# Second attention started while the experts run: tiles by rank of rows, results stored in place

## The chip, the cores and the metric

One core of a Trainium2 chip runs one program: TensorE (PE), VectorE (DVE), ScalarE (ACT), GpSimd (POOL) and the DMA queue engine SP. The metric is device time in microseconds; the kernel before took 1532.71 us (median of 3 runs, 1528.11 to 1534.6).

## The reference, cut to what matters

The input is 16 batches of 256 tokens of 128 numbers, all float32. Four blocks, each followed by a residual sum and a layer norm:

```
x = LN(x + attention0(x))    # MLP, 16 heads of 64, softmax over keys j < i + 64, output projection
x = LN(x + experts(x))       # 16 experts of 128 -> 512 -> 128 with exact gelu, top 4 of 16 per token
x = LN(x + attention1(x))    # 16 heads of 8, LoRA-corrected q, k, v, o; keys of the own batch
x = LN(x + gated(x))         # per batch t: f, i = sigmoid, g = tanh of x_t and state c;
                             # c = f*c + i*g over t = 0..15; h = tanh(x_t wo + c_final uo + bo)
```

The router's logits are minus the squared distance to 16 keys plus a linear term; the weights of the four best are a softmax over them. The state c (256 x 128) is carried over all 16 batches, and the last block's output needs the final c for every batch.

## The kernel before, in words

All of it is one program with an instruction stream for each engine, written out by hand; semaphores (`need`, `need_alone`, `wait_ge`) set the order. It has four stages.

**First attention** (loops over 16 batches x 8 pairs of heads, `body(b)` of each engine). When a batch is normed, DVE routes it: `pos` is the row of `xs` (in HBM; a region of CAP = 4224 rows for each expert) of each of the token's four copies, and POOL scatters the 256 x 4 rows there with eight indirect DMAs (L515). SP fills `xs` with zeros beforehand.

**Experts.** Once all rows are scattered, DVE makes a plan (L1284 to L1315): 144 tiles of 128 rows, all tiles of expert 0 first, then those of expert 1, and so on. For tile n, SP loads the rows (L408), PE transposes them (L850), DVE copies that expert's weights out of `wall` (L1348, L1351) and the transposed rows out of PSUM (L1355), PE does the first layer (L864), ACT the gelu (L1076), PE two tiles later the second layer (L873), DVE adds the bias (L1376), SP stores pairs of tiles to `ys` (L414). The loop has a body of 24 tiles (TURN), five of them straight code and three passes of a loop in the middle. POOL meanwhile shifts all positions from regions to plan order (L552 to L566), clears the stacks and builds constants, each piece released by a tile (`next_tile`).

**Second attention** (`attention_loop`: bodies b = -3 to 17, the middle ones in a loop of three). Body b works on several batches at once: POOL gathers batch b+5 (eight indirect DMAs, L614), ACT weighs batch b+4 (L1136), POOL sums it (L640 to L644), DVE norms batch b+3 (`norms_start`, `norms_end`), PE projects batch b+2 to q and k (L925, L926), which are split in three bf16 parts (`parts`) and sent by SP through HBM (`qkd`, L439) into stacks `qst`, `kst` (L447 to L451), PE computes scores of batch b+1 (L967) for their row maxima (L1389), and of batch b transposed, with the maxima as further rows of the stack (L892), of which ACT takes the exponential (L1086) and PE the product with v (L904). The maxima travel as `mrow` (ACT L1141), then by a DMA of SP into 24 rows of the stack (L459), once for each half of the heads: half 1 is needed at the body's pair p = 4, half 0, sent at p = 5 of the body before, at its first pair. Batch b-1 gets its output projection and norm, batch b-2 its gates (L983 to L987), and POOL updates the state (L650 to L656).

**Tail.** PE multiplies the last state (L994), DVE adds it and POOL a quarter (L1477, L677), ACT takes tanh in four groups of four batches (L1151), DVE and POOL add the residual (L1484, L681), DVE and POOL compute the last norm's moments, ACT scales (L1156) and SP writes out.

## Time and profile before

| | |
|---|---|
| median of 3 runs | 1532.71 us |
| profiled execution | 1530.1 us, span 1528.3 us |
| busy share PE, DVE, ACT, POOL | 83%, 66%, 61%, 52% |
| mean granted TensorE clock | 0.93 |
| mean DMA | 76 GB/s, 115.51 MB |

The profile's times count from the start of the span. An engine's idle time is put down to what released it; "issue" is time in which it waited for nothing that the profile shows. A line such as L864 is a line of the kernel. `wall` as a target in the second attention is the third stack and the exponentials: they lie in the place of the experts' weights.

### The profile page before, as it was taken

The page shows a single profiled execution, that of the slowest core. Times are in us where ns is not written, and L with a number is a line of the kernel's source. Part 1 is how long each engine was busy: PE and PEld are TensorE (multiplying, and loading weights), DVE is VectorE, ACT ScalarE, POOL GpSimd, SP SyncE. Part 2 cuts the span into 40 slices and gives each one's busy share as a digit, 9 for nine tenths or more (in the row PEclk, how much of TensorE's full clock was granted, in tenths as well). Part 3 has the DMA queues.
Part 4 walks back from the last instruction along what each step waited for, and adds up shares of the span by engine and source line. Part 5 has one row for each costly group of instructions (what it writes and reads, how often), then busy time and mean ns, then how long its engine had stood idle before and what let it go on. Part 6 is the DMA issues. An engine that isn't in the chain of part 4 may idle for free.

```text
span 1528.3 us, 36861 instructions
## 1 busy us (share of the span) xinstructions
PE 1270.1 (83%) x9712; PEld 970.9 (64%) x9712; DVE 1011.6 (66%) x3751; ACT 939.1 (61%) x2828; POOL 796.6 (52%) x1025
## 2 busy tenths in 40 slices
PE   7999999999999999856999889803768787878870
PEld 3776767777777776646999889801445554555540
DVE  2677777777777777755776657514677776668726
ACT  5877777777777777624665456412555655656544
POOL 1557777777777777743332100175456665653133
PEclk9999999999999999978999999955899999999995
DMA  9522222222222222112222122115343435343201
GB/s 345 171 60 70 69 67 67 69 69 69 69 69 69 69 69 69 44 51 58 72 69 70 58 61 70 56 45 92 82 86 74 94 66 91 68 88 57 46 4 55
DMA packets 150448, 115.51 MB, mean 76 GB/s; under 512 B 11809, under 2 KB 139937, under 8 KB 148290
## 3 DMA queue, kind: packets, MB, share of 16 engines
q1 hardware_dynamic: 142146, 97.50, 24.9%
q0 software_dynamic: 8192, 16.79, 4.2%
q8 instruction: 39, 0.64, 0.2%
q14 instruction: 71, 0.58, 0.1%
HBM read 50.02 MB, written 61.08 MB: 73 GB/s over the span
## 4 chain that ended last, share of the span: by engine, by line
PE 29%; DMA 7%; DVE 5%; issue 4%; DVEq 3%; POOL 2%; ACT 2%; another core or an unknown queue 2%; SPq 1%; POOLq 1%; ACTq 0%
PE psum L864 8%; PE psum L873 8%; DMA qst<-mrow 3%; DMA wall<-mrow 3%; PE psum L904 2%; PE psum L892 2%; PE psum L967 2%; POOL yk L614 1%; PE psum L983 1%; PE psum L850 1%; DVE mx L1389 1%; PE psum L984 1%; ACT wall L1086 1%; DMA yk<-ys,posc 1%
## 5 line engine op out<-in xcount | busy, mean ns | idle before, releaser
L525 POOL TENSOR_SCALAR P<-P,rinv 128x192 f32<-128x192 f32 (+1 forms) x384 | 309.4, 820 | 154.1 <-DVE rinv L1216 151.7
L1051 ACT ACTIVATE P<-shifted,least 128x192 f32<-128x192 f32 (+1 forms) x512 | 240.2, 471 | 103.2 <-DVE least L1202 101.8
L1076 ACT ACTIVATE hid<-psum,wA 128x128 f32<-128x128 f32 x576 | 164.7, 369 | 118.9 <-PE psum L864 118.9
L1389 DVE TENSOR_REDUCE mx<-psum 128x2 f32<-128x512 f32 x256 | 165.0, 686 | 83.4 <-PE psum L967 56.1
L1086 ACT ACTIVATE wall<-psum 128x1024 f32<-128x1024 f32 x128 | 131.1, 1024 | 98.9 <-PE psum L892 81.7
L1202 DVE CUSTOM_DVE_ANT_0 shifted<-psum,band 128x192 f32<-128x192 f32 (+1 forms) x512 | 168.7, 384 | 26.0 <-PE psum L749 25.7
L864 PE MATMUL psum<-xgT,wA 128*128 128x128 f32 x1152 | 155.8, 279 | 8.9 <-DVE xgT L1355 8.8
L515 POOL DMA_INDIRECT xs<-x1c,pos x128 | 128.2, 1001 | 56.8 <-issue 28.3
L873 PE MATMUL psum<-wB,hid 128*128 128x128 f32 x1152 | 153.5, 277 | 0.0
L614 POOL DMA_INDIRECT yk<-ys,posc x128 | 124.2, 970 | 55.7 <-issue 29.0
L864 PEld LDWEIGHTS psum<-xgT,wA 128*128 128x128 f32 x1152 | 143.4, 196 | 9.6 <-issue 9.5
L873 PEld LDWEIGHTS psum<-wB,hid 128*128 128x128 f32 x1152 | 141.5, 194 | 0.0
L786 PEld LDWEIGHTS psum<-ident,P 128*128 128x128 f32 x1024 | 117.0, 141 | 36.3 <-issue 29.4
L786 PE MATMUL psum<-ident,P 128*128 128x128 f32 x1024 | 134.9, 274 | 3.7 <-POOL P L525 1.5
L749 PE MATMUL psum<-kT,qT 64*128 64x192 f32 (+1 forms) x1024 | 131.5, 375 | 0.6 <-DVE least L1202 0.6
L804 PE MATMUL psum<-PT,V 128*64 128x256 f32 (+1 forms) x1024 | 112.2, 362 | 0.7 <-DVE PT L1190 0.7
L749 PEld LDWEIGHTS psum<-kT,qT 64*128 64x128 f32 x1024 | 80.2, 186 | 38.6 <-issue 36.9
L1348 DVE COPY wA<-wall 128x516 f32 x144 | 61.9, 430 | 64.4 <-ACT hid L1076 41.5
L1051 ACT ACTIVATION_READ_ACCUMULATOR P<-shifted,least 128x1 f32 x512 | 95.9, 187 | 0.0
L1190 DVE COPY PT<-psum 128x448 f32<-128x448 f32 x128 | 79.0, 618 | 17.1 <-PE psum L804 7.8
L697 PE MATMUL psum<-hT,wg 128*128 (+1 forms) x256 | 88.9, 429 | 1.7 <-ACT kT L1008 0.9
L804 PEld LDWEIGHTS psum<-PT,V 128*64 128x64 f32 x1024 | 68.5, 138 | 30.9 <-issue 9.0
(243 smaller groups left out, 2550.7 us busy)
## 6 DMA issues: line engine op xcount, KB each, us to landing
xs<-zrow SPq DMA_DIRECT2D x33, 1024.0 KB
xg<-xs SPq DMA_DIRECT2D x144, 64.0 KB, 1.8
ys<-yrow SPq DMA_DIRECT2D x72, 128.0 KB, 1.9
wall<-in_wall SPq DMA_DIRECT2D x1, 8232.0 KB, 36.5
qkd<-parts SPq DMA_DIRECT2D x32, 192.0 KB
qst<-qkd SPq DMA_DIRECT2D x66, 64.0 KB
wall<-qkd SPq DMA_DIRECT2D x35, 64.0 KB
kst<-qkd SPq DMA_DIRECT2D x11, 192.0 KB
```

The costliest lines, as they stand in the source:

```text
L525: g.tensor_scalar(x, x, rinv[:, par, n:n + 1], None, ALU.mult).then_inc(s["pn_ready"], 1)
L614: g.indirect_dma_start(out=yk[:, slot, count * half + n, :], out_offset=None, in_=ys, in_offset=bass.IndirectOffsetOnAxis(posc[:, half, n: ...
L749: last = mm(bk[:, c0:c0 + w], qT[64 * h:64 * h + 64, p, it * 128:(it + 1) * 128], kT[64 * h:64 * h + 64, p, 0:w], start=True, stop=True)
L786: last = nc.tensor.transpose(bk[:, c0:c0 + 128], P[:, par1, it, h, jt * 128:(jt + 1) * 128], ident[:, :])
L804: last = mm(OTB[64 * h:64 * h + 64, k * N + c0:k * N + N], V[:, jt, r * 128 + 64 * h:r * 128 + 64 * h + 64], PT[:, k, h, keys], start=(jt ...
L864: mm(UP[two][:, at:at + GT], wA[:, p % 4, f * 128:(f + 1) * 128], xgT[:, p % 4, :], start=True, stop=True).then_inc(s["up_mm"], 1)
L873: last = mm(DN[two][:, 0:D], hid[:, m, f, :], wB[:, m, f * D:(f + 1) * D], start=(f == 0), stop=(f == FC - 1))
L1051: last = sc.activation(P[:, par, it, h, 0:w], shifted[:, par, it, h, 0:w], ACT.Exp, scale=-1.0, bias=least[:, par, n:n + 1], accum_out=row ...
L1076: sc.activation(hid[:, p % 4, f, :], UP[two][:, at:at + GT], ACT.Gelu, bias=wA[:, p % 4, F + f:F + f + 1]).then_inc(s["hid_ready"], 1)
L1086: sc.activation(pc[:, p % 4, :, :, :].rearrange("q h j n -> q (h j n)"), ST, ACT.Exp, scale=SCALE1).then_inc(s["exps1"], 1)
L1202: v.tensor_tensor_reduce(out=shifted[:, par, it, h, 0:w], in0=bk[:, c0:c0 + w], in1=band[:, it, 0:w], scale=-SCALE0, scalar=3.0e38, op0=AL ...
L1389: v.tensor_reduce(out=mx[:, :, h], in_=SB[(par + 1 + h) % 3].rearrange("q (i n) -> q i n", i=TT), axis=mybir.AxisListType.X, op=ALU.max).t ...
```

## The change

What it does, by part:

- The plan goes by rank: first the first tile of every expert, then every second tile, and so on (`upto`, `level`, `order`). Rows no longer change place: results are stored into the rows of `xs` that were read, tile by tile, and `pos` is used as it is; POOL's shift of positions is gone. Empty tiles get rows of their own behind the regions.
- The experts' loop is straight code of 144 tiles. Their hidden layer takes three PSUM banks in turn instead of four (`up`), which frees bank 7.
- During the experts POOL gathers batches 0 to 3 (once 32, 64, 96 and 128 tiles are stored), ACT weighs and POOL sums batches 0 to 2, DVE norms batches 0 and 1, PE transposes them and projects batch 0, and SP loads its stack. The second attention then begins with body -1 instead of -3.
- Before the experts: no barrier of four engines; the last batch's rows go to `h1` instead of `x1c`; its pow stands ahead of two scatters; ACT loads the table of gelu early.
- In the second attention the DMA of `mrow` is issued by ACT, in `maxima_row`; `parts` go out in four DMAs of 64 partitions instead of two of 128; the transposes of x2 and x3 stand behind the last scores of a body; POOL adds `bo2` to each batch's output rows.
- Tail: for the last two batches DVE updates the state; the last gates compute the part without c ahead; output rows are put into PSUM by an identity matmul and the state's part is added there, tanh reads PSUM; the last scaling is shared by ACT and DVE.

The diff, cut to its core:

```diff
-TURN = 24
-NT += -NT % TURN
-ROWS = DUMMY + GT
+NT += NT % 2
+FULL = TOK * TOPK // GT
+ROWS = DUMMY + (NT - FULL) * GT
+LEVELS = TOK // GT
...
+        def up(n, f):
+            return bank[(2 * n + f // 2) % 3][:, (f % 2) * GT:(f % 2 + 1) * GT]
...
+            def store_rows(n):
+                need_alone(sp, "yrow_ready", n + 1)
+                need_alone(sp, f"ys_out{n % 2}", 16 * (n // 2))
+                sp.dma_start(xs[bass.ds(row[n], GT), :], yrow[:, n % 4, :]).then_inc(s[f"ys_out{n % 2}"], 16)
...
+            sp.wait_ge(s["scat"], 16 * B * TT * TOPK)
+            for n in range(NT + 4):
+                if n + 4 < NT:
+                    load_rows(n + 4)
+                if n >= 4:
+                    store_rows(n - 4)
+                if n == 95:
+                    store_parts(-2)
...
+                if n in (98, 100, 102):
+                    load_stack(-2, 0, (n - 98) // 2)
...
-            for e in range(E):
-                for half in (slice(0, npos // 2), slice(npos // 2, npos)):
-                    next_tile()
-                    g.tensor_scalar(shift[:, half, e], posf_all[:, half], first_row[:, e:e + 1], delta[:, e:e + 1], ALU.is_ge, ALU.mult)
...
+            stored(32)
+            fetch(-5, -5 % 3, 0)
+            fetch(-5, -5 % 3, 1)
+            combine_ahead(-4, 60)
+            stored(64)
...
+            stored(128)
+            fetch(-2, -2 % 3, 0)
+            fetch(-2, -2 % 3, 1)
             pool.wait_ge(s["wB_ready"], NT)
             clear(2)
             select_copy(2)
             g.drain().then_inc(s["cleared"], 1)
-            pool.wait_ge(s["ys_out"], 8 * NT)
+            stored(NT)
...
+            for n in range(NT + 2):
+                tile(n)
+                if n == 82:
+                    attention(-3, -3 % 3, (7,))
+                if n == 86:
+                    attention(-2, -2 % 3, (1,))
+                if n == 116:
+                    attention(-2, -2 % 3, (7,))
...
                 need_full(act, b, use)
                 sc.activation(mrow[:, half, :], shared(use).bitcast(bf16)[0:NMAX, 0:N], ACT.Copy).then_inc(s[f"free{use[0]}"], 1)
...
+                act.dma_start(qst[slot][MROW:MROW + NMAX, half * hh:half * hh + hh, :],
+                              mrow[:, half, :].rearrange("q (o n) -> q o n", o=1).to_broadcast([NMAX, hh, N])).then_inc(s["mrow_in"], 16)
...
+            for n in range(NT):
+                tile(n)
+                if 50 <= n < 58:
+                    weigh_ahead(-4, n - 50)
+                if n == 83:
+                    attention(-3, -3 % 3, (7,))
+                if 85 <= n < 93 and n != 87:
+                    weigh_ahead(-3, n - 85 - (n > 87))
...
-            v.tensor_tensor_scan(ncum[:, :], past[:, :], ntile[:, :], 0.0, ALU.mult, ALU.add)
+            v.tensor_tensor(lesser[:, :, :], ntile[:, :].rearrange("q (o e) -> q o e", o=1).to_broadcast([128, LEVELS, E]),
+                            levels[:, :].rearrange("q (l o) -> q l o", o=1).to_broadcast([128, LEVELS, E]), ALU.min)
+            v.drain()
+            v.tensor_reduce(out=upto[:, :], in_=lesser[:, :, :], axis=mybir.AxisListType.X, op=ALU.add)
...
+            for n in range(NT + 2):
+                tile(n)
+                for b, first in ((-3, 70), (-2, 104)):
+                    if n == first:
+                        norms_start(b)
...
+            def state_in(c):
+
+                wo3 = gu[:, 3, :].rearrange("q (o d) -> q o d", o=1).to_broadcast([128, 2, D])
+                for half in range(2):
+                    for it in range(TT):
+                        last = mm(bank[2 * c + half].rearrange("q (k i d) -> q k i d", k=2, i=TT)[:, :, it, :], c2[:, it * 128:(it + 1) * 128], wo3, start=False, stop=(it == TT - 1))
+                last.then_inc(s["h_full"], 1)
```

The change moves instructions; three places show how. First SP in the second attention, one body that loads a stack (`qkd` is the split q and k in HBM, `mrow` the row maxima, `wall` here the third stack). Before:

```order
L439 DMA qkd<-parts 128x3x256 x2
L447 DMA kst<-qkd 24x4096
L449 DMA qst<-qkd 8x4096 x3
L447 DMA kst<-qkd 16x4096
L449 DMA qst<-qkd 8x4096 x2
L447 DMA kst<-qkd 8x4096
L449 DMA qst<-qkd 8x4096
L451 DMA qst<-zeros 24x4096
L459 DMA wall<-mrow 24x8x256 x2
```

And now:

```order
L440 DMA qkd<-parts 64x3x256 x4
L451 DMA kst<-qkd 24x2x2048
L453 DMA qst<-qkd 8x2x2048 x3
L451 DMA kst<-qkd 16x2x2048
L453 DMA qst<-qkd 8x2x2048 x2
L451 DMA kst<-qkd 8x2x2048
L453 DMA qst<-qkd 8x2x2048
L455 DMA qst<-zeros 24x2x2048
```

The two DMAs of `mrow` have left SP's queue, and the parts go out in four. Second, ACT in a body of the second attention, from the exponential of pair 4 on (`tf`, `ti` are gates, `yk` the gathered rows that it weighs). Before:

```order
L1108 ACTIVATE tf<-psum,gcol 128x256
L1109 ACTIVATE ti<-psum,gcol 128x256
L1086 ACTIVATE wall<-psum 128x1024
L1141 ACTIVATE mrow<-psum 24x256
L1086 ACTIVATE wall<-psum 128x1024
L1090 ACTIVATE oTc<-psum 128x256
L1112 ACTIVATE tg<-psum,gcol 128x256
```

And now:

```order
L1206 ACTIVATE tf<-psum,gcol 128x256
L1207 ACTIVATE ti<-psum,gcol 128x256
L1185 ACTIVATE wall<-psum 128x1024
L1237 ACTIVATE mrow<-psum 24x256
L1240 DMA qst<-mrow 24x8x256
L1185 ACTIVATE wall<-psum 128x1024
L1189 ACTIVATE oTc<-psum 128x256
L1210 ACTIVATE tg<-psum,gcol 128x256
```

The DMA of `mrow` stands on ACT behind the copy that makes it. Third, PE in the experts around tile 82 (L913 is the first layer, L924 the second, L1004 the transposes of batch 0's norm). Before, the tiles go on unbroken:

```order
L864 MATMUL psum<-xgT,wA 128x128 x4
L850 MATMUL psum<-ident,xg 128x128
L873 MATMUL psum<-wB,hid 128x128 x4
L864 MATMUL psum<-xgT,wA 128x128 x4
L850 MATMUL psum<-ident,xg 128x128
L873 MATMUL psum<-wB,hid 128x128 x4
```

And now:

```order
L913 MATMUL psum<-xgT,wA 128x128 x4
L901 MATMUL psum<-ident,xg 128x128
L924 MATMUL psum<-wB,hid 128x128 x4
L1004 MATMUL psum<-ident,x2c 128x128 x2
L913 MATMUL psum<-xgT,wA 128x128 x4
L901 MATMUL psum<-ident,xg 128x128
L924 MATMUL psum<-wB,hid 128x128 x4
L913 MATMUL psum<-xgT,wA 128x128 x4
```

The transposes, which opened the second attention before, stand between two tiles.

## Rows read from the trace of the kernel before

**Rows 1.** The page, part 2: granted TensorE clock in 40 slices.
```profile
PEclk9999999999999999978999999955899999999995
```

**Rows 2.** Busy time by stretch of the whole core (from:to, length, then as headed).
```profile
core 0: us, PE busy (x) PEld busy (x) DVE busy (x) ACT busy (x) POOL busy (x), PEclk, DMA share, GB/s
835.00:850.00 15.00, 10.34 (x74) 10.16 (x73) 6.71 (x21) 4.68 (x16) 2.91 (x6) 0.77 0.15 45
850.00:885.00 35.00, 35.00 (x316) 35.00 (x316) 23.70 (x72) 21.45 (x76) 2.37 (x5) 1.00 0.23 68
885.00:905.00 20.00, 15.90 (x128) 15.72 (x128) 10.43 (x33) 8.40 (x30) 0.00 (x0) 0.91 0.18 52
988.00:1044.00 56.00, 3.40 (x8) 1.76 (x8) 7.72 (x26) 7.49 (x24) 38.21 (x50) 0.54 0.28 60
1044.00:1068.00 24.00, 10.70 (x45) 5.05 (x46) 17.20 (x38) 6.58 (x19) 13.51 (x17) 0.64 0.45 84
1067.90:1452.80 384.90, 306.55 (x2544) 204.32 (x2544) 275.19 (x824) 224.46 (x442) 198.79 (x268) 0.92 0.39 74
```

**Rows 3.** Timeline before the first tile (start, length, engine, line, operation, idle).
```profile
672.48 0.75 POOL L506 TENSOR_TENSOR rstd<-veps,minus_half 128x2 f32<-128x2 f32 x1
...
674.41 0.60 DVE L1262 TENSOR_SCALAR x1c<-res,mv,rstd 128x128 f32<-128x128 f32 x2 [0.52 <-DMA xs<-x1c,pos]
...
692.10 0.96 POOL L515 DMA_INDIRECT xs<-x1c,pos  x1 [0.30 <-issue]
...
699.97 1.94 PE L864 MATMUL psum<-xgT,wA 128*128 128x128 f32 x8
...
701.13 1.28 ACT L1076 ACT_TABLE_LOAD   x1 [13.90 <-PE psum L864]
```

**Rows 4.** Timeline from the last tile to the first scores.
```profile
987.94 0.29 DVE L1376 TENSOR_TENSOR yrow<-psum,wB 128x128 f32<-128x128 f32 x1 [0.60 <-PE psum L873]
...
1044.01 1.04 PE L967 MATMUL psum<-kst,qst 128*128 128x256 bf16 x4 [6.40 <-DMA qst<-zeros]
```

**Rows 5.** Timeline of PE: starts of seven bodies of the second attention.
```profile
1067.94 1.04 PE L892 MATMUL psum<-qst,kst 128*128 128x256 bf16 x4 [6.90 <-DMA qst<-mrow]
...
1172.74 0.61 PE L892 MATMUL psum<-qst,kst 128*128 128x256 bf16 x4 [1.34 <-ACT wall L1086]
...
1197.24 0.61 PE L892 MATMUL psum<-wall 128*128 128x256 bf16 x4 [1.36 <-ACT wall L1086]
...
1223.10 1.03 PE L892 MATMUL psum<-qst,kst 128*128 128x256 bf16 x4 [3.65 <-DMA qst<-mrow]
...
1303.85 0.61 PE L892 MATMUL psum<-qst,kst 128*128 128x256 bf16 x4 [1.22 <-ACT wall L1086]
...
1331.08 0.61 PE L892 MATMUL psum<-qst,kst 128*128 128x256 bf16 x4 [1.22 <-ACT wall L1086]
...
1452.84 0.60 PE L892 MATMUL psum<-qst,kst 128*128 128x256 bf16 x4 [0.33 <-ACT wall L1086]
```

**Rows 6.** Timeline of SP: three issues in the second attention.
```profile
1208.88 0.33 SPq L447 DMA_DIRECT2D kst<-qkd  x1
...
1212.95 0.84 SPq L459 DMA_DIRECT2D qst<-mrow  x1
...
1447.93 9.41 SPq L459 DMA_DIRECT2D qst<-mrow  x2
```

**Rows 7.** The page, part 6: KB each, median us to landing.
```profile
xg<-xs SPq DMA_DIRECT2D x144, 64.0 KB, 1.8
ys<-yrow SPq DMA_DIRECT2D x72, 128.0 KB, 1.9
```

**Rows 8.** Timeline of the tail.
```profile
1489.42 0.41 POOL L650 TENSOR_SCALAR tf<-tf 128x256 f32<-128x256 f32 x1 [5.75 <-ACT tg L1112]
...
1493.11 1.22 PE L994 MATMUL psum<-gu,c 128*128 128x128 f32 x4 [4.40 <-POOL c L656]
...
1500.52 1.21 DVE L1484 TENSOR_TENSOR x_all<-x_all,wall 128x1024 f32<-128x1024 f32 x1
```

More of the change, by code:

```diff
@@ L69, in attention_loop @@
 def attention_loop(eng, body):
-    for b in range(-3, 3):
+    for b in range(-1, 3):
         body(b, b % 3)
@@ L416, in _ @@
[L416 to L427 removed]
+                row[n] = row_of(n)
@@ new lines, in load_stack @@
+            def load_stack(b, load, qa):
+                if qa == 0:
+                    need_alone(sp, "qkd_out", 64 * (b + 3))
+                    need_alone(sp, "st_full", 8 * b)
+                rows = [qkd[w].rearrange("e a (d h) n -> (a d) e (h n)", h=H1 // 2) for w in range(2)]
+                q, k = [x[load].rearrange("q (e h) n -> q e (h n)", e=2) for x in (qst, kst)]
+                count = NPART - qa
+                n = sum(NPART - c for c in range(qa))
+                sp.dma_start(k[DH1 * n:DH1 * (n + count), :, :], rows[1][0:DH1 * count, :, :]).then_inc(s["stk"], 16)
+                for m in range(count):
+                    sp.dma_start(q[DH1 * (n + m):DH1 * (n + m + 1), :, :], rows[0][DH1 * qa:DH1 * (qa + 1), :, :]).then_inc(s["stk"], 16)
+                if qa == NPART - 1:
+                    sp.dma_start(q[MROW:MROW + NMAX, :, :], no_maxima).then_inc(s["stk"], 16)
@@ L883, in attention @@
+            def attention(b, par, steps=range(8)):
                 nxt = (par + 1) % 3
-                for p in range(8):
+                for p in steps:
                     if has(b, 0):
@@ new lines, in outputs_in @@
+            def outputs_in(c):
+                need(pe, "xo_kept", 4 * (c + 1))
+                if c == 0:
+                    need(pe, "exps1", 8 * B)
+                if c in (1, 2):
+                    need(pe, "max_done", H1 * B)
+                if c == 2:
+                    need(pe, "o_free", 4 * B)
+                    need(pe, "to_free", 4 * B)
+                if c == 3:
+                    for k in range(2):
+                        need(pe, f"free{k}", tally[k].before(B + 2))
+                for half in range(2):
+                    mm(bank[2 * c + half][:, :], ident[:, :], xo_all[:, 8 * c + 4 * half:8 * c + 4 * half + 4, :].rearrange("q t d -> q (t d)"), start=True, stop=False)
@@ L1121, in attention @@
                         if has(b, 3):
-                            last = sc.activation(x2T[:, par, :], shared(TX)[:, 0:N], ACT.Copy)
+                            last = sc.activation(x2T[:, par, :], shared(TX, b)[:, 0:N], ACT.Copy)
                         if has(b, -1):
-                            last = sc.activation(x3T[:, :], shared(TX)[:, N:2 * N], ACT.Copy)
+                            last = sc.activation(x3T[:, :], shared(TX, b)[:, N:2 * N], ACT.Copy)
                         last.then_inc(s[f"free{TX[0]}"], 1)
-                    if p == 7 and isinstance(b, int) and b == -3:
-                        for half in range(2):
-                            weigh(b, par, half)
             def weigh(b, par, half):
@@ L1457, in attention @@
                         norms_start(b)
+                        norms_spread(b)
                     if p == 6 and (has(b, 3) or has(b, -1)):
                         norms_end(b)
+                        norms_out(b)
                     if p == 2 and has(b, 2):
-                        need(dve, "a1_ready", b + 3)
-                        v.tensor_tensor(rest[:, :], shared(QK)[:, :], parts[:, 0, :], ALU.subtract).then_inc(s[f"free{QK[0]}"], 1)
+                        for k in range(3):
+                            parts_of(b, k)
```

659 lines of the change are left out of this document (359 added, 300 removed).

## Prediction

> **What bounds the kernel now.** I read the busy slices and the clock row first, then busy time by stretch, then timelines of the stretches in which TensorE idles, and last the issue table. The clock row shows two dips, at slices 18 (the hand-over to the experts) and 27 to 29 (from the experts to the second attention) [rows 1]. TensorE does the experts at full rate: 316 instructions in 35.00 us is 9.03 per us; a tile is 17 instructions (two times 4 matmuls of two passes, one transpose), so 1.88 us, and 144 tiles are 271 us [rows 2]. Two stretches fall short: 74 instructions in 15 us and 128 in 20 us [rows 2]. From 988 to 1044 us TensorE runs 8 instructions, POOL is busy 38.21 us [rows 2]: the gathers. So the kernel is four stages in series, each with another limit: the first attention (not changed), the experts (TensorE), the second attention (no engine over 306.55 of 384.90 us [rows 2], a ring of waits), and a tail on DVE and ACT. The change works on the seams and on the ring of waits.
>
> The sum is made against the profiled execution, 1530.1 us with a span of 1528.3. The median shown is 1532.71, within 0.2% of it, so I give the sum as the forecast.
>
> **Before the first tile.** The last batch's pow stood on POOL behind two scatters of batch 14 that now follow it. One scatter is 0.96 us and a gap of 0.30 [rows 3], so 2.5 us sooner; the pow ended at 673.2 and DVE wrote x1c at 674.41 with 0.52 us idle for scatters that still read x1c [rows 3], which goes too, since these rows now go into h1. Positions are released before gates are written, about 0.5 more. From the end of the last scatter, 693.06, to the first tile's matmul at 699.97 are 6.9 us [rows 3]. They held the landing, a four-engine barrier, DVE's small set-up, weight copies and a load of rows (1.8 us [rows 7]). The barrier, set-up and weight copies are now done while scatters run; left are the landing (some 1.3 us), the load, a transpose and a copy (some 1 us), about 4.2, so 2.7 saved. The Gelu table load of 1.28 us [rows 3] now comes before. Sum 7.5. DVE's plan has grown by a minimum and a reduction of 512 elements each and two or three steps, perhaps 2.5 us, under 10 us of scatters; it costs nothing while the scatters end last. Ends: 4 (the plan's two DMAs come last) and 10. I take 7.5.
>
> **The experts.** At 9.03 per us the two short stretches lack (135 - 74) and (181 - 128) instructions: 6.8 and 5.8 us, 12.6 in all [rows 2]. They lie where the loop of 24 tiles jumps back (tiles 72 and 96), the stretches of straight code on either side have none, and the changed program is straight code. So 12.6 can go. Against that: on TensorE two pairs of transposes and one QK projection (about 2 us at the rate of [rows 2]); on ACT 24 weightings, two evacuations of x2T, one of parts; on DVE two norms and three splits. ACT was busy 21.45 of 35.00 us and DVE 23.70 [rows 2], 0.73 and 0.61 us free in each tile, and the work is spread one piece to a tile. TensorE's new wait in mid tile is for the first half of the tile before, which ACT ended over a microsecond earlier. SP now stores each tile alone and in place and loads one stack for the second attention in three parts; the row loads queue behind each part. They are asked for about three tiles (5.6 us) ahead and land in 1.8 [rows 7], so I allow 1 us a part. Net gain 12.6 - 2 - 3 = 7.6. Ends: 0 and 12.6. The order by rank changes no count: 144 tiles in both.
>
> **Between experts and second attention.** Last row of the experts 987.94 (end 988.2), first scores 1044.01 [rows 4], first exponentials' matmul 1067.94, 6.90 of which it waited for a DMA of row maxima [rows 5]. So 80 us. In between came the gather, norm, projection and stacking of the first batch, which are now done during the experts; left is the body b = -1, which ran from 1044.01 to 1067.94 less the wait, 17.0 us. That body's maxima are sent at its p = 5 and needed only when the next body begins. But batch 1 is still projected in that body: its stack was loaded from 11.6 us after a body's start (1208.88 against 1197.24 [rows 5, 6]) and cannot have landed much before 1223.10, 25.9 after it, because the maxima behind it landed only then; the next body's first scores want it at about 19. I charge 3 of these 7 us, because part of them is the maxima's own transfer. Gain 80 - 17 - 3 = 60. Ends: 53 and 64.
>
> **The loop of the second attention.** From 1067.94 to 1452.84 are 15 bodies of 25.66 us [rows 5]. The row maxima's DMA was issued at 1212.95, right behind the stack's, and TensorE got it at 1223.10, 10.2 us later, having idled 3.65; then it ran at the lower level (four matmuls in 1.03 us where others take 0.61) for some 5 us, worth 2 more [rows 5, 6]. The last such DMA with no stack ahead of it was issued from 1447.93 and at 1452.84 nobody waited for it [rows 5, 6]: under 4.9 us. Issued by ACT, on another queue, it should land before TensorE asks. Yet bodies that do not wait for it are no shorter: 1172.74 to 1197.24 is 24.5 us, 1303.85 to 1331.08 is 27.2 [rows 5]. There DVE, ACT and TensorE wait for one another, and a stall lets the late ones catch up, so most of the wait comes back elsewhere. Floor: TensorE's own 306.55 / 15 = 20.4 us; with DVE's and POOL's hand-overs I can't see it under 22.5. Roof: 25.7 or a little above, since ACT issues two DMAs a body of 0.84 us each [rows 6] (behind it stand the copy of parts for DVE and the next exponential), and POOL gets an addition of 256 elements. For it: the transposes of x2 and x3 now stand behind the last scores, so DVE's last maxima no longer wait for ACT. I take 24.0, near the 24.5 of the best undisturbed body: 15 x 1.66 = 25. Ends: 0 and 47.
>
> Here the Trainium skill speaks against the change: "DMA: Bandwidth & Descriptors", section "Issuing engines are not separate DMA queues", says that DMAs of several issuers run on the same 16 engines and that a second issuer saves only the time of issuing. By that the move would save the queueing of 0.84 us of issue and the loop gains nothing: 1449. The same page ("Queues, rings and completion order") says each engine takes turns between the rows of its queues, so a short transfer can overtake a long one; by that the sum stands. No row here has a DMA from ACT.
>
> **The tail.** For the last two batches the state is updated by DVE: POOL took from 1489.42 to 1493.11, 3.7 us; three DVE operations of 256 elements, where 1024 take 1.21 [rows 8], are some 1.3. That would be 4.8 for two, but TensorE gets four identity matmuls of 512 columns between the gates of batch 14, which give some 4 back (an estimate from four matmuls of 256 bf16 columns in 0.61 to 1.03 us [rows 5], at a few times the passes); the last gates have their x3 half done early (about 1). From 1493.11, when the state is known, to DVE's first sum at 1500.52 are 7.4 us [rows 8]; adding the state in PSUM and tanh straight from it needs about two matmul pairs and one activation, 3.1. The fourth sum returns from POOL to DVE, and the last scaling is shared: even. Net 7.4 - 3.1 + 4.8 - 4 + 1 = 6. Ends: 1 and 10.
>
> **Sum.** 7.5 + 7.6 + 60 + 25 + 6 = 106; 1530.1 - 106 = 1424.
>
> **Rivals.**
> - The stack is next (the ring stays as slow): bodies stay at 25.7 because the stack's landing, or the hand-overs, take the place of the maxima. For it: the bodies without that wait are as long as the others [rows 5]. Against it: the wait costs clock as well. 1424 + 25 = 1449. It is also what the first rule above gives.
> - The ring opens: 22.5 us a body, 15 x 1.5 = 22 less: 1402. For it: TensorE is free of its longest wait at full clock. Against it: ACT's extra 1.7 us.
> - The lead inside the experts is too short: ACT stands at a weighting until its gather lands, or TensorE at row loads behind a stack part. Three sets, 4 to 5 us each beyond what I allowed: 1437. For it: POOL issues 8 gathers in front of each set, at 1.26 us each if they go like the scatters [rows 3]. Against it: 5 to 12 tiles lie between.
> - Slower: SP's store waits until the store two tiles before has landed. With 1.9 us [rows 7] that is free; it decides the tile's time once a landing takes over two tiles, 3.8 us, and the tile is then half a landing. To eat 106 us over 144 tiles it must be 0.74 us more a tile, a landing of 5.2 us on average. Nothing in the rows points there (the largest transfers share the engines for three tiles only): then 1531 and above.
> - The change doesn't do what it says (early batches' rows lie in later tiles): a batch has 256 tokens, so at most two tiles of rows for each of 16 experts, 32 tiles. Excluded by count.
>
> **Numbers.** Forecast 0.43, ring as slow 0.20, ring opens 0.18, short lead 0.14, slower 0.03, the rest spread over sums of the ends 0.02. The likeliest is 1424, its own range 1410 to 1438. The range that should hold 8 in 10 takes both loop cases and half of the other ends: 1396 to 1454. Under 0.5% (7.6 us), about what a measurement of this kernel can tell from no change, nothing could be said; only the slower rival comes near or beyond: faster 0.97, within 0.5% 0.01, slower 0.02.
>
> **What would show it.** Right: first tile at about 692; the last tile's end near 973 with the instruction rate of TensorE never far below 9 per us; the second attention's first scores within 1 us of that, its first exponential's matmul about 20 us later; no idle of TensorE for mrow; bodies near 24; from the last state to the end about 31 us. Wrong: dips in TensorE's rate near tiles 50, 85, 98 to 104 or 119; TensorE idle for the stack (kst, qst from qkd) at a body's first scores; bodies at 25.7 with no DMA wait; gaps before the first tile ended by the plan.

## The result and the profile after

The changed kernel takes 1485.86 us (median of 4 runs, 1481.32 to 1487.53) against 1531.7 of the kernel before in the same comparison: ratio 0.9697, 95% interval 0.9666 to 0.9729. The prediction was 1424 with a range of 1396 to 1454. The sign was right, the size was not: 46 us came of 106.

The profiled execution has a span of 1479.6 us (1528.3 before). It was the shortest of the four, 4.5 us under their median, so the stages below add up to a few us less than a usual run of this kernel. Where the 48.7 us between the two spans are, stage by stage (starts of TensorE's matmuls, from the rows below and [rows 3, 4, 5, 8]):

| stage | before | after | change | predicted |
|---|---|---|---|---|
| start to first tile | 699.97 | 691.51 | -8.5 | -7.5 |
| experts | 288.0 | 304.4 | +16.4 | -7.6 |
| to the first exponential's matmul | 80.0 | 15.6 | -64.4 | -60 |
| 15 bodies of the second attention | 384.9 (25.66 each) | 398.2 (26.54 each) | +13.3 | -25 |
| from there to the end | 75.5 | 69.9 | -5.6 | -6 |

Three terms held within 5 us. Two stages, the experts and the loop, came out longer than before where I had them shorter, by 24 and 38 us. Timeline of the changed kernel, PE at the borders of the stages and DVE in the tail:

```profile
691.51 0.76 PE L913 MATMUL psum<-xgT,wA 128*128 128x128 f32 x2 [0.43 <-DVE xgT L1482]
...
995.87 0.60 PE L1020 MATMUL psum<-kst,qst 128*128 128x256 bf16 x4
...
1011.50 1.03 PE L937 MATMUL psum<-qst,kst 128*128 128x256 bf16 x4 [0.91 <-DMA qst<-mrow]
...
1409.66 0.49 PE L937 MATMUL psum<-qst,kst 128*128 128x256 bf16 x3 [0.33 <-ACT wall L1185]
...
1448.05 5.39 PE L1080 MATMUL psum<-gu,c 128*128 128x256 f32 x16 [2.52 <-DVE c L1614]
...
1452.87 1.22 DVE L1636 TENSOR_TENSOR x_all<-x_all,wall 128x1024 f32<-128x1024 f32 x1 [4.88 <-ACT wall L1272]
```

The first scores follow the last tile with no gap, 4.8 us lie between the last state and DVE's first sum (7.4 before, [rows 8]), and the end is 31.5 us behind the last state (35.2 before), as forecast.

Busy time by stretch of the changed kernel: one plain stretch of the experts, then the four in which TensorE's count of instructions falls, then the loop (columns as in [rows 2]):

```profile
core 0: us, PE busy (x) PEld busy (x) DVE busy (x) ACT busy (x) POOL busy (x), PEclk, DMA share, GB/s
705.00:725.00 20.00, 20.00 (x182) 20.00 (x181) 14.72 (x43) 12.44 (x44) 5.43 (x10) 1.00 0.24 71
765.00:785.00 20.00, 17.06 (x139) 16.58 (x138) 10.64 (x31) 9.12 (x32) 9.12 (x13) 0.91 0.29 80
825.00:845.00 20.00, 15.36 (x117) 14.63 (x115) 10.19 (x32) 7.97 (x28) 8.78 (x11) 0.91 0.29 79
895.00:925.00 30.00, 24.68 (x198) 23.73 (x198) 17.01 (x51) 13.20 (x47) 10.26 (x14) 0.94 0.46 103
965.00:985.00 20.00, 15.72 (x121) 15.15 (x120) 10.00 (x28) 8.09 (x28) 8.98 (x12) 0.91 0.29 82
1011.50:1409.60 398.10, 308.11 (x2544) 203.26 (x2544) 278.67 (x828) 220.37 (x443) 212.17 (x283) 0.91 0.39 74
```

The clock row of the page (as [rows 1]):

```profile
PEclk9999999999999999996999999996999898999997
```

The hand-over to the experts still shows (slice 18), the long dip at 5 behind them is one slice at 6. A plain stretch has 182 instructions in 20 us. The four lack 43, 65, 75 and 61: 244, or 26.8 us at 9.1 per us. Before, the two dips at the loop's jumps cost 12.6 us; 26.8 less 12.6 and 2 us for the moved matmuls make the 16.4 of the table. In each of the four POOL is the one engine that does more than in the plain stretch (about 9 us in 20 in place of 5.4, in the third 10.26 in 30): that is where it issues its sets of eight gathers. TensorE's instructions in the loop are the same 2544 as before [rows 2], and no engine's busy time explains 13 us: TensorE's is 1.6 us longer, POOL's 13.4, but POOL idles for 186 of the 398 us, and in experiment 8 it is as busy (211.5 us) in a loop of 384.0. The engines waited more for each other and for DMAs.

### The profile page after: what moved, and what is told of

Same layout as the page of the kernel before. It is cut to its first block, busy times and chain, and to the rows that moved or that the text cites. A ratio compares the mean times of both kernels' runs of the same rounds, so it can differ in the third digit from the quotient of the medians.

```text
span 1479.6 us, 36706 instructions
## 1 busy us (share of the span) xinstructions
PE 1284.3 (87%) x9756; PEld 978.9 (66%) x9756; DVE 1011.3 (68%) x3763; ACT 931.6 (63%) x2825; POOL 773.2 (52%) x991
## 4 chain that ended last, share of the span: by engine, by line
PE 59%; DVE 11%; issue 8%; DMA 7%; ACT 5%; another core or an unknown queue 3%; SPq 3%; DVEq 3%; ACTq 1%; POOL 0%; POOLq 0%
PE psum L913 9%; PE psum L924 8%; PE psum L800 6%; PE psum L837 6%; PE psum L855 5%; PE psum L748 4%; DMA qst<-mrow 3%; PE psum L817 3%; PE psum L755 3%; PE psum L949 3%; PE psum L749 2%; PE psum L937 2%; DMA qst<-zeros 2%; ACT P L1155 2%
## 5 line engine op out<-in xcount | busy, mean ns | idle before, releaser
L913 PE MATMUL psum<-xgT,wA 128*128 128x128 f32 x1152 | 160.3, 282 | 13.7 <-ACT hid L1177 9.6
L913 PEld LDWEIGHTS psum<-xgT,wA 128*128 128x128 f32 x1152 | 146.0, 198 | 16.8 <-ACT hid L1177 11.2
L924 PE MATMUL psum<-wB,hid 128*128 128x128 f32 x1152 | 155.2, 279 | 0.0
L598 POOL DMA_INDIRECT yk<-xs,posc x128 | 125.9, 984 | 55.6 <-issue 32.5
L924 PEld LDWEIGHTS psum<-wB,hid 128*128 128x128 f32 x1152 | 142.9, 195 | 0.0
L543 POOL DMA_INDIRECT xs<-x1c,pos x120 | 120.3, 1002 | 39.0 <-issue 35.1
L800 PEld LDWEIGHTS psum<-kT,qT 64*128 64x128 f32 x1024 | 80.2, 186 | 38.6 <-issue 36.9
L1311 DVE COPY PT<-psum 128x448 f32<-128x448 f32 x128 | 79.0, 617 | 17.1 <-PE psum L855 7.3
L1478 DVE COPY wB<-wall 128x640 f32 x144 | 73.7, 512 | 20.9 <-DVE yrow L1504 1.5
```

The source lines that it names most:

```text
L800: last = mm(bk[:, c0:c0 + w], qT[64 * h:64 * h + 64, p, it * 128:(it + 1) * 128], kT[64 * h:64 * h + 64, p, 0:w], start=True, stop=True)
L913: mm(up(n, f), wA[:, n % 4, f * 128:(f + 1) * 128], xgT[:, n % 4, :], start=True, stop=True).then_inc(s["up_mm"], 1)
L924: last = mm(DN[n % 2][:, 0:D], hid[:, m, f, :], wB[:, m, f * D:(f + 1) * D], start=(f == 0), stop=(f == FC - 1))
```

## The experiments

All times are medians; "changed" is the changed kernel (1485.9), "before" the kernel before (1529 to 1532 in these comparisons). Two profiled executions of like kernels differ by a few us, so only differences above some 5 us are read. The kernels were measured in several comparisons, each with its own runs of the kernel before. A difference of two medians can therefore be some us off what the ratios to before say: the 17 us of experiment 8 are 12 by the ratios, the 30 of experiment 7 are 27, the 36.5 of experiment 12 are 31.5, the 16 of experiment 1 are 18.

**1. No gathers in the experts.** Edit to the changed kernel, with the waits for them turned to the fills:

```diff
                     for n in range(begin, end):
+                        if isinstance(b, int) and b < -1:
+                            last = g.memset(yk[:, slot, count * half + n, :], 0.0)
+                            if n == end - 1:
+                                last.then_inc(s["yk_set"], 1)
+                            continue
```

> The changed kernel, but the four sets of eight gathers that POOL issues while the experts run are left out (small fills of the same rows stand in their place, so the first four batches attend over zeros); weighings, norms, projection and stack stay where they are. In the changed kernel TensorE issues 92 instructions per 10 us in the experts, except in 765 to 785 (140), 825 to 845 (120), 895 to 925 (200) and 965 to 985 (123): 44 + 64 + 76 + 61 = 245 short of 92 per 10 us, 26.6 us. Theory 'the gathers hold up the tiles': all four dips but the part of the third that is the stack's (some 4 us) go, the time from the first tile to the first scores falls from 304.3 to about 281 and the kernel by 22 to 26 us, to about 1462. Rival 'the work moved in (weighings on ACT, norms on DVE, stack on SP) costs the time': the dips stay, under 5 us of change.

Measured 1469.5 (ratio to before 0.9579, 0.9534 to 0.9624): 16 us. First tile to first scores is 286.4 us in place of 304.4. Busy time by stretch:

```profile
765.00:785.00 20.00, 20.00 (x182) 20.00 (x181) 14.87 (x43) 12.24 (x44) 3.47 (x14) 1.00 0.24 71
825.00:845.00 20.00, 20.00 (x182) 20.00 (x181) 14.99 (x50) 11.73 (x42) 0.86 (x1) 1.00 0.24 69
880.00:910.00 30.00, 23.48 (x190) 22.72 (x190) 17.13 (x51) 12.70 (x45) 5.00 (x15) 0.94 0.40 92
955.00:975.00 20.00, 20.00 (x182) 20.00 (x181) 14.87 (x43) 11.77 (x42) 3.55 (x12) 1.00 0.22 62
```

Three dips are gone. The other one stays as large as it was and now lies a little earlier, where the stack is loaded: 273 instructions would be full, 190 ran, 9 us are lost (8 before this edit). The weighings, norms and splits still run, at full rate of TensorE.

**2. One gather per tile.**

```diff
                     for n in range(begin, end):
+                        if isinstance(b, int) and b < -1:
+                            at_tile(32 * (b + 5) + (38 if b < -2 else 36) + 4 * half + n)
```

> The changed kernel, but in the experts POOL waits for a new tile ahead of each of its gathers: one gather per tile of 1.9 us, where now eight follow each other every 1.25 us. Theory 'gathers back to back hold up the tiles, because the row loads and stores of SP stand between them': with 1.9 us each, every load has a gap, each set costs at most 1 us in place of 5 to 8, the kernel gains 15 to 22 us, about 1468. Rival 'each gather costs a fixed time wherever it stands' (26.6 us over 32 gathers, 0.8 us each): no change, 1486.

Measured 1467.4 (0.9582, 0.9556 to 0.9608): 18.5 us, as much as with no gather at all. First tile to first scores 283.7 us. Stretches of this kernel, the first under the first set of gathers, the last where the stack is loaded:

```profile
765.00:785.00 20.00, 19.56 (x175) 19.37 (x174) 13.52 (x41) 11.66 (x42) 9.13 (x13) 1.00 0.31 89
835.00:855.00 20.00, 20.00 (x182) 20.00 (x181) 15.00 (x48) 11.86 (x42) 6.44 (x8) 1.00 0.34 91
880.00:910.00 30.00, 24.86 (x219) 24.29 (x218) 19.49 (x58) 14.80 (x52) 10.07 (x14) 1.00 0.46 109
```

The first stretch lacks 7 instructions, 0.8 us, and the dip at the stack has 54 in place of 75. So it is neither the count of gathers nor their work that costs, but that eight of them follow each other. In the profiles of experiments 1 to 3 the loop behind takes 400 to 407 us in place of 398; the figures for the experts' stage do not contain that.

**3. Plain DMAs of the same bytes in place of the gathers.**

```diff
+                        if isinstance(b, int) and b < -1:
+                            at = ((b + 5) * 8 + count * half + n) * 128
+                            g.dma_start(yk[:, slot, count * half + n, :], t["x"][at:at + 128, :]).then_inc(s[f"yk_in{half}"], 16)
+                            continue
```

> The changed kernel with the 32 gathers that POOL issues in the experts replaced by 32 plain DMAs on the same queue of POOL, back to back, of the same 64 KB each and into the same rows, from the input x (the first four batches attend over other rows; this leaves out their gathering). Theory 'traffic: what SP's rows share with the transfers costs the time': the dips stay, 1482 to 1488. Rival 'it is the gather itself (the work of issuing by index, row by row), not its bytes': the dips go as they did with the gathers left out, about 1468.

Measured 1467.1 (0.9573, 0.9534 to 0.9612). Timeline of POOL and busy time by stretch of this kernel, then two gathers of the changed kernel:

```profile
768.54 2.54 POOL L600 DMA_DIRECT2D yk<-in_x  x4 [0.66 <-POOL posc L595]
```

```profile
765.00:785.00 20.00, 20.00 (x182) 20.00 (x181) 14.99 (x44) 11.70 (x42) 6.15 (x13) 1.00 0.34 100
825.00:845.00 20.00, 20.00 (x182) 20.00 (x181) 14.89 (x50) 12.36 (x44) 3.76 (x7) 1.00 0.34 95
```

```profile
769.82 0.96 POOL L598 DMA_INDIRECT yk<-xs,posc  x1 [0.30 <-issue]
771.09 0.94 POOL L598 DMA_INDIRECT yk<-xs,posc  x1 [0.30 <-issue]
```

The plain ones bring the same 64 KB every 0.6 us, twice as fast as the gathers, at 100 GB/s in place of 80, and TensorE loses nothing. From 700 to 980 us POOL's queue carries the same in both kernels, 1024 packets and 2.10 MB. So the amount of traffic is excluded; what is left is the gather as an operation, or that it reads scattered rows of `xs`, where the plain DMAs read `x` in order: no run separates these two. How it holds up the others is not settled. The waits in a dip look like this (changed kernel, PE, then ACT):

```profile
835.77 0.61 PE L913 MATMUL psum<-xgT,wA 128*128 128x128 f32 x4
840.14 0.96 PE L913 MATMUL psum<-xgT,wA 128*128 128x128 f32 x4 [3.77 <-ACT hid L1177]
```

```profile
833.81 0.87 ACT L1177 ACTIVATE hid<-psum,wA 128x128 f32<-128x128 f32 x3
839.47 1.66 ACT L1177 ACTIVATE hid<-psum,wA 128x128 f32<-128x128 f32 x6 [4.79 <-remote]
```

TensorE waits for ACT, and ACT starts at 839.47 on matmuls that the profile has done by 836.4; "remote" is its word for a release that it can't name. In the same dip DVE starts its copy of transposed rows at 839.60, also from "remote". It is as if signals between engines came late while gathers were issued. A rival is that the straight code itself is loaded late: an instruction packet runs at 838.9, just ahead of these starts, but none in the 2 us ahead of the end of the like stall of ACT and DVE at 979. No run here shows more.

**4. The kernel before, experts as straight code.**

```diff
+def straight(body):
+
+    for i in range(NT // TURN + 1):
+        body(i)
...
-            batch_loop(pe, 2, NT // TURN - 1, 2, tiles)
+            straight(tiles)
```

> The kernel before with nothing changed but the experts' loop of 24 tiles written out as straight code of 144 tiles on SP, PE, ACT and DVE. Theory of my prediction: the two stretches in which TensorE fell short, 12.6 us, were the jumps back in the loop; they go, 1519. Rival: straight code is fetched too, and something is lost evenly or at other places: 1527 to 1532.

Measured 1522.4 against 1531.7 (0.9943, 0.9922 to 0.9965): 9 us; from the first tile's to the last tile's matmuls 271.9 us in place of 285.1. The two stretches that fell short [rows 2] are full:

```profile
835.00:855.00 20.00, 20.00 (x182) 20.00 (x181) 14.78 (x44) 11.73 (x43) 5.86 (x11) 1.00 0.23 68
885.00:905.00 20.00, 20.00 (x182) 20.00 (x181) 14.88 (x43) 12.47 (x44) 0.00 (x0) 1.00 0.25 73
```

**5. Row maxima's DMA back on SP** (`spread_maxima` of the kernel before in place of the issue in `maxima_row`).

> The changed kernel with the DMAs of the row maxima back on SP, at the same two places of its program as in the kernel before. In the changed kernel TensorE still waited for this DMA in nine bodies (up to 4.84 us), a body took 26.5 us on average against 25.7 before. Theory A 'the transfer, not the issue queue, is late: the 16 engines carry the stack': back on SP the waits are about the same or a little longer, the body within 0.5 us of 26.5; total 1480 to 1495. Theory B 'the move to ACT made the bodies longer, since ACT spends 0.8 us on each issue and queues its exponentials behind': back on SP the bodies return to 25.7, total about 1473. Theory C (my prediction's step): the move helped and other parts of the change lost it: the total rises by 10 us or more.

Measured 1486.9 (0.9710, 0.9684 to 0.9736), a body 26.8 us, waits for `mrow` in 12 of 16 bodies, 45.9 us in all where changed has 26.8 in 10: theory A, though the waits are more than a little longer.

**6. The same edit alone on the kernel before.**

> The kernel before with one change, the DMA of the row maxima issued by ACT behind its copy instead of by SP. My prediction priced this edit at 15 x 1.66 us, 25 us: 1507. The run with the DMA put back on SP in the changed kernel lost 1 us, so theory A 'the transfer is late on any queue' says 1525 to 1535 and waits for the row maxima of the same size as before (10 of them, 1.6 to 6.9 us).

Measured 1532.7 against 1530.4 (1.0010, 0.9990 to 1.0029), a body 25.56 us in place of 25.66. The edit that I priced at 25 us is worth nothing that can be told in either kernel (here between 4.4 us lost and 1.5 gained). One expectation missed: the waits for the row maxima did not keep their size, they fell from 36.4 us (10 of them) to 20.5 (7):

```profile
PE psum L888 <- DMA qst<-mrow: 10.9, 4, 3.9
PE psum L888 <- DMA wall<-mrow: 9.6, 3, 4.5
```

So the move takes 16 us of these waits away here, and 19 between experiment 5 and changed: about 1 us a body, where one issue takes 0.8. Yet the bodies are 0.1 and 0.3 us shorter: the time comes back as other waits. In the 15 bodies here, those for what ACT writes into `wall` (the exponentials above all) went from 12.9 to 17.1 us, those with no releaser (issue) from 4.7 to 9.8.

**7. A quarter of the stack's bytes.**

```diff
-                sp.dma_start(k[DH1 * n:DH1 * (n + count), :, :], rows[1][0:DH1 * count, :, :]).then_inc(s["stk"], 16)
+                sp.dma_start(k[DH1 * n:DH1 * (n + count), :, 0:512], rows[1][0:DH1 * count, :, 0:512]).then_inc(s["stk"], 16)
```

(and so for q and the zeros)

> The changed kernel with every load of the stack (k, q and the zeros for the row maxima) cut to a quarter of its bytes, the number of DMAs and their order kept; the rest of the stack stays as it was, so scores are those of stale rows. This leaves out part of the loading. Theory A of the row maxima 'they land late because the 16 engines carry the stack': the waits for the row maxima (10 of them, 25.8 us in all in the changed kernel) fall below 5 us in all, and bodies to 25 or less: 1450 to 1465. Rival 'their latency is their own (24 rows read once, written 8 times)': the waits stay as long, total within 4 us of 1486.

Measured 1455.4 (0.9523, 0.9490 to 0.9555): 30 us less than changed, and a body 24.29 us. What TensorE waited for in the loop, longest first (total, times, longest), in the changed kernel:

```profile
PE psum L937 <- DMA qst<-mrow: 20.8, 8, 4.5
PE psum L1020 <- DVE mx L1514: 12.4, 12, 2.5
PE psum L937 <- ACT wall L1185: 11.2, 10, 1.7
PE psum L1028 <- ACT ti L1207: 10.1, 9, 2.6
PE psum L1020 <- DMA qst<-zeros: 7.9, 3, 5.6
PE psum L949 <- DVEq L1598: 6.0, 18, 0.5
PE psum L937 <- DMA wall<-mrow: 6.0, 2, 4.8
```

and with a quarter of the bytes (no row of a DMA is left), with its busy row, the DMA share 0.20 in place of 0.39:

```profile
PE psum L937 <- ACT wall L1185: 20.0, 16, 2.4
PE psum L1020 <- DVE mx L1514: 15.7, 13, 2.9
PE psum L1028 <- ACT ti L1207: 10.9, 8, 1.9
```

```profile
1014.20:1378.50 364.30, 299.67 (x2545) 200.70 (x2543) 284.08 (x830) 222.40 (x444) 211.56 (x284) 0.95 0.20 51
```

The row maxima come late because the DMA engines are carrying the stack. The packets show it. q10 is the queue of ACT's DMAs, q1 that of SP's; a DMA of the maxima is 204 packets. In the changed kernel, for the one issued at 1328.46, in 1328.4:1334, 1334:1336.9 (no packet of q10) and 1336.9:1339.4:

```profile
q10 hardware_dynamic: 68, 0.03, 5.6%
q1 hardware_dynamic: 65, 0.19, 52.4%
q10 hardware_dynamic: 136, 0.07, 15.6%
```

and with a quarter of the bytes, for one issued at 1311.52, in 1311.4:1314:

```profile
q10 hardware_dynamic: 204, 0.10, 18.8%
```

Some packets of the maxima run among the stack's, from 1.5 to 3 us behind the issue, but the last ones only about when the stack's end: 7.7 to 9.7 us behind the issue in twelve bodies of the changed kernel, 2.3 to 3.4 with a quarter of the bytes. That is also what the Trainium skill says ("DMA: Bandwidth & Descriptors", section "Issuing engines are not separate DMA queues"): DMAs of several issuers run on the same engines, and only the time of issuing is saved. By that rule the trace agrees: its own queue saved the maxima about one issue a body (experiment 6), and the transfer as a whole did not overtake the stack's.

**8. The old way into the stack.** Parts in two DMAs of 128 partitions, heads interleaved as before, loads of one block of 4096 columns:

```diff
-                    for e in range(2):
-                        sp.dma_start(qkd[w, e].rearrange("a r n -> r a n"), parts[64 * e:64 * e + 64, :, w * N:(w + 1) * N]).then_inc(s["qkd_out"], 16)
+                    sp.dma_start(qkd[w].rearrange("a r n -> r a n"), parts[:, :, w * N:(w + 1) * N]).then_inc(s["qkd_out"], 16)
```

> The changed kernel with the way into the stack as in the kernel before: parts in two DMAs of 128 partitions instead of four of 64, the heads' layout that goes with it. Median over bodies 2 to 11: parts are sent 9.4 us after a body's start in both kernels, the first stack load is issued at 12.2 us before and at 14.1 now, the last at 15.5 to 16.4 before and at 17.2 now. Theory 'the four smaller DMAs land later, so the stack and the row maxima that share the engines with it come later': undone, the bodies return to about 25.7, gain 10 to 13 us, about 1474. Rival 'the stack's start has slack': no change, 1486.

Measured 1469.2 (0.9620, 0.9579 to 0.9661): 17 us, a body 25.60 us. Timeline of one body, DMA issues (SPq, ACTq) and TensorE's release, changed kernel:

```profile
1320.61 2.49 SPq L440 DMA_DIRECT2D qkd<-parts  x4
1325.23 0.30 SPq L451 DMA_DIRECT2D kst<-qkd  x1
...
1328.34 0.37 SPq L455 DMA_DIRECT2D qst<-zeros  x1
1328.46 0.80 ACTq L1240 DMA_DIRECT2D qst<-mrow  x1
...
1339.36 1.04 PE L937 MATMUL psum<-qst,kst 128*128 128x256 bf16 x4 [4.53 <-DMA qst<-mrow]
```

and with the old way:

```profile
1284.37 0.91 SPq L439 DMA_DIRECT2D qkd<-parts  x2
1287.19 0.31 SPq L450 DMA_DIRECT2D kst<-qkd  x1
...
1290.76 0.37 SPq L454 DMA_DIRECT2D qst<-zeros  x1
...
1293.10 0.80 ACTq L1239 DMA_DIRECT2D wall<-mrow  x1
```

From the issue of the parts to the first stack load are 4.6 us with four DMAs and 2.8 with two (medians of the loads in the profiles: 4.5 and 3.0). Nearly all of the difference is SP's time of issuing, 2.49 us for four and 0.91 for two; from the last issue's end to the load it is 2.1 and 1.9. In the changed kernel the maxima go out 0.1 us behind the last stack load and are there 10.9 us later, on a queue of their own; in the kernel before it took 10.2, behind the stack on SP [rows 5, 6].

**9. Old layout and loads, but four DMAs of parts.** Experiment 8 with its two DMAs split again:

```diff
-                    sp.dma_start(qkd[w].rearrange("a r n -> r a n"), parts[:, :, w * N:(w + 1) * N]).then_inc(s["qkd_out"], 16)
+                    for e in range(2):
+                        sp.dma_start(qkd[w][:, 64 * e:64 * e + 64, :].rearrange("a r n -> r a n"), parts[64 * e:64 * e + 64, :, w * N:(w + 1) * N]).then_inc(s["qkd_out"], 16)
```

> The changed kernel with the stack's loads and the heads' layout as in the kernel before, but the parts sent in four DMAs of 64 partitions as now. With both undone it took 1469. Theory 'four DMAs land later than two': about 1484, a body 26.5. Rival 'the shape of the loads (two blocks of 2048 columns in place of one of 4096) or the layout costs it': 1469, a body 25.6.

Measured 1477.1 (0.9652, 0.9620 to 0.9684), a body 26.44 us: between the two. Against the version with two DMAs a body is 0.84 us longer, so the four DMAs cost 8 us by the medians (5 by the ratios, whose intervals overlap) and 12.6 by the loops of the profiles. TensorE's waits for `mrow` are 38.6 us with four and 27.0 with two, those for the zeros, the stack's last load, 5.3 and 1.2. Changed, however, waits no longer for `mrow` than the version with two DMAs (26.8), only for the zeros (7.9): that the stack starts later is shown, how this makes the body longer only in part. The other 9 us between this and changed lie in no one stage (experts 3.7, loop 1.5), and half of them in none, as changed's profile is 4.5 us under its median; what of them is the layout stays open.

**10. Transposes of x2 and x3 ahead of the last scores again.**

> The changed kernel with the transposes of x2 and x3 back ahead of the last scores of a body, from body -1 on. Theory 'the new place makes bodies longer': ACT copies x2T and x3T ahead of the next body's first exponential, and these copies now come behind TensorE's last scores, which wait for DVE's maxima; put back, the bodies return from 26.5 towards 25.7, the kernel gains 8 to 13 us, about 1475. Rival, my prediction's step (the new place frees DVE's last maxima from ACT): put back, the kernel loses 3 to 10 us, 1489 to 1496. No effect within 3 us: the place is indifferent, and the longer bodies come from elsewhere.

Measured 1486.0 (0.9728, 0.9687 to 0.9769), a body 26.62: indifferent, within what the two intervals leave open (some 5 us).

**11. No gather at all in the second attention.**

> The changed kernel without any gather of the second attention, neither in the experts nor in its bodies (fills of the same rows on POOL stand in their place, so every batch attends over zeros): this leaves out the fetching of the experts' results. Bodies 4 to 12 of the changed kernel, with eight gathers each, take 27.5 us, bodies 13 to 15, which have none, 25.0, 24.5 and 20.8. Theory 'gathers back to back hold up TensorE, ACT and DVE in the bodies as they do in the experts': bodies with gathers left out fall to 25 or below, 12 bodies by 2.5 us are 30 us, with the 16 us that leaving them out in the experts brought: about 1440. Rival 'the bodies are bound by the stack's transfer and the hand-overs, and gathers are hidden': bodies stay within 0.5 us of 26.5, total about 1468.

Measured 1447.4 (0.9450, 0.9413 to 0.9486). A body takes 25.5 us, 1.0 less, not the 2.5 of the theory, and bodies 13 and 14, which I had taken for short because they lack gathers, take 26.8 and 25.4 here, so that was not the reason. TensorE now waits for `mrow` in 15 bodies, 1 to 4.5 us each: behind the gathers stands the same late transfer.

**12. A better version: one gather per tile and the old way into the stack** (edits 2 and 8).

> A version meant to be better: one gather per tile in the experts (measured at 1467.4) and the way into the stack as in the kernel before. If the stack's way costs 10 to 13 us in the bodies, 1456; if it is indifferent, 1467.

Measured 1449.3 (0.9491, 0.9453 to 0.9530), 36.5 us faster than the changed kernel. First scores at 974.67 (I had forecast 973 for the last tile's end), a body 25.47. This beats both kernels.

**13 and 14. Two attempts beyond it.** In the first, the gathers of the second attention are spread too:

> As the version with one gather per tile and the old way into the stack, and in the second attention the second and third gather of the second set of four wait for the next exponential each, which puts some 2.5 us between them in place of 1.25 (POOL has 4.3 us idle behind them). Theory 'gathers back to back hold up the other engines in the bodies too' (without any gather a body took 25.5 in place of 26.6): half of 1.1 us a body comes back for half of the gathers, 5 to 8 us less than the version without this. Rival 'in the bodies it is the gathers' traffic or POOL's time, not their spacing': no change, or 3 to 8 us more because POOL's pow comes later.

Measured 1453.8 (0.9509, 0.9482 to 0.9535), a body 25.94: no gain. In the second, the stack's ten loads in the experts go one a tile:

> A version meant to be the best: one gather per tile and the old way into the stack (measured at 1449.3), and the first stack's ten loads in the experts one per tile from tile 98 on instead of in groups of four, three and three. TensorE falls 58 instructions short of 92 per 10 us in 880 to 910 in the version with spaced gathers, 6.3 us, and waits there 4.7 us for the rows of two tiles. Theory 'the row loads queue behind a group of stack loads': 4 to 6 us gained, 1444. Rival 'the stack's bytes cost that wherever they lie': 1449.

Measured 1451.9 (0.9476, 0.9446 to 0.9506): no gain that can be told. From 870 to 930 us TensorE lacks 56 instructions of 546, where it lacked 53 with groups: the price is not their grouping. Nor is it shown to be their bytes: with a quarter of these (experiment 7, gathers in a row) it lacks 99 in the same stretch, and 83 in changed. What it is stays open; TensorE waits there for rows (`xg`), 3 to 6 us in each of these kernels.

## Why the prediction was wrong

- **Before the first tile, prologue, tail.** Right: -8.5, -64.4 and -5.6 against -7.5, -60 and -6. Before the first tile that is partly luck: the last scatter ended 6.8 us sooner (686.29 against 693.06) where my terms for it make 3.5, and from there to the first tile 1.7 us were saved where I had 4.0. The tail held term by term: 1.9 us up to the last state (1.8 forecast), 3.6 behind it (4.3). Part of the prologue's gain was given back in the loop: its first body took 31.4 us, in which TensorE waited 5.62 us for the stack of batch 1; I had charged 3.
- **The experts, the term "12.6 can go".** Right: straight code alone gives 9 us by the medians, 13.2 by the stage (experiment 4).
- **The experts, the term of 3 us "against that".** This failed. The sum has no term for the gathers: I priced them by POOL's time alone, in a rival, and asked only what the row loads would meet. Three of the four dips come from eight gathers in a row (experiments 1 to 3), 18 to 21 us of the stage with what the set at the stack may add, and the stretch with the stack's loads lost 6 to 9 in place of 3. The rival "lead too short" named the right stage with 13 us. Its part on row loads that wait behind the stack was seen (TensorE waited for `xg` there), its main part was not: in the four dips ACT's waits are put to TensorE or "remote", never to a gather's data.
- **The loop, the term "issued by ACT, on another queue, it should land before TensorE asks".** This failed. The landing took 10.9 us on ACT's queue, 10.2 on SP's, since the stack's bytes held it (experiment 7). The move saved about one issue a body of waiting, and that came back at other waits (experiments 5, 6), as my own reading of the ring had said it would. The rule of the Trainium skill that I set beside the sum, and the rival of 0.20 that goes with it, had this step right; the loop then came out 13 us above that rival too, by the next point. My price for a body without the wait was near, 24.0 against 24.3 with a quarter of the stack's bytes, though that run has less traffic as well as no wait. The edit just doesn't remove it.
- **The loop, the edit that I didn't price.** Four DMAs of parts in place of two start the stack 1.5 to 1.8 us later in a body and cost 5 to 13 us (experiments 8, 9). I read that the parts "go out in four" and took it for even.
- **The transposes behind the last scores.** I counted this for the loop; it is indifferent (experiment 10).
- **In-place stores** were free, as I had it under the rival "slower": outside the stack's loads TensorE keeps 175 to 182 instructions in 20 us with spaced gathers. The order by rank and the stores by single tiles cost nothing that can be seen.

By terms: +16.4 in the experts is -13 for straight code, +18 to 21 for back-to-back gathers, +6 to 9 for the stretch with the stack's loads and +2 or so for the moved matmuls (my estimate, not measured alone); +13.3 in the loop is +14 for the way into the stack by the profiles (of it 4.5 in the first body, 31.4 against 26.9), and nothing for the rest.

## What to carry to other kernels

Moving a DMA to another engine's queue bought the issue time alone here, and not even that in the total: when the transfer is late, look at what else the 16 engines carry at that moment, and cut or delay that. Work put beneath a saturated engine must be priced by what it does to the others: beneath the experts eight indexed DMAs of POOL in a row cost 5 to 7 us, eight with a tile between them under 1. In the second attention, where no engine is saturated, spreading some of them gained nothing (experiment 13). Splitting a transfer that another waits for doubles its issues and can delay everything behind it: price each edit to a chain of DMAs, however small, by the time from its first issue to the next issue that waits for it.

## What the runs showed of the hardware

A gather of 64 KB took 1.25 us from issue to issue on POOL, a plain DMA of the same size on the same queue 0.6, and in the experts only the gathers in a row slowed PE, ACT and DVE. The granted clock was 0.91 in three of the dips and 0.94 in the one at the stack, where it is 1.00 in a plain stretch. So a dip costs its idle time and some matmuls at the lower of the two levels, 1.2 GHz, behind it: after the wait of 3.77 us the four at 840.14 took 0.96 us, the four at 835.77 before it 0.61. Packets of two queues ran in the same stretch, and yet the last ones of 96 KB that were issued behind the stack ran only about when the stack's ended, 7.7 to 9.7 us behind the issue (experiment 7). A jump back in a loop of 24 tiles cost TensorE about 6 us each of the two times it is seen, and 144 tiles of straight code cost nothing that can be seen.
